# Mamba stage on one core: the two silu activations in one ScalarE block, and the convolution products, norm, gate, residual and output products at other units of the loop body

## What is computed

```python
xz = jnp.einsum('bsd,ed->bse', x, ip_w)
xi, z = jnp.split(xz, 2, axis=-1)
conv = conv_general_dilated(xi.transpose(0, 2, 1), cw, ...) + cb
xi = silu(conv.transpose(0, 2, 1))
dt, Bm, Cm = jnp.split(jnp.einsum('bse,fe->bsf', xi, xp_w), ...)
dt = softplus(jnp.einsum('bsr,er->bse', dt, dtp_w) + dtp_b)
def step(h, t):            # h = exp(dt*A) * h + dt*B*xi,  y = sum_s h*C
    ...
y = ys + xi * Dp
y = y * silu(z)
return jnp.einsum('bse,de->bsd', y, op_w)
```

## Time and profile before

| | value |
|---|---|
| median of three runs | 7089.75 us |
| the profiled execution's own time | 7097.04 us |
| its span | 7095.2 us |
| TensorE, share of the span busy | 88% |
| GpSimd | 66% |
| VectorE | 73% |
| ScalarE | 53% |
| granted TensorE clock, mean | 0.945 of full speed |
| one body of Mamba (36 of them, about 58% of the span) | 114.67 us |

### The profile page before, as it was taken

How to read it: one execution, slowest core, us unless ns; L and a number is a source line. 1 busy time by engine, 2 the same in 40 slices (tenths; PEclk the granted TensorE clock), 3 DMA queues, 4 the chain that set the end, 5 groups by cost and what they waited for, 6 DMA issues and landing times. The chain is left out here.

```text
span 7095.2 us, 72243 instructions
## 1 busy us (share of the span) xinstructions
PE 6238.9 (88%) x19866; PEld 2543.6 (36%) x19866; DVE 5157.7 (73%) x6021; ACT 3746.3 (53%) x6881; POOL 4712.5 (66%) x2193
## 2 busy tenths in 40 slices
PE   8999999999899888889888888888898888888898
PEld 3444444455344233323233322333222333223334
DVE  4444444454222999999999999999999999995623
ACT  4444444422223666666666666666666666664432
POOL 3333333311200999999999999999999999993300
PEclk9999999999999999989899989999898989999998
DMA  2000000100200332324233333323242333332000
GB/s 71 0 0 0 0 0 0 51 10 9 102 0 22 77 82 63 84 72 94 66 82 73 74 95 73 81 64 84 61 105 65 82 73 76 80 82 54 5 0 24
DMA packets 235643, 378.46 MB, mean 53 GB/s; under 512 B 62784, under 2 KB 71680, under 8 KB 233776
## 3 DMA queue, kind: packets, MB, share of 16 engines
q1 hardware_dynamic: 235312, 374.71, 21.7%
HBM read 202.29 MB, written 19.20 MB: 31 GB/s over the span
## 5 line engine op out<-in xcount | busy, mean ns | idle before, releaser
L2413 POOL TENSOR_TENSOR work<-work,weights 128x1024 f32<-128x1024 f32 x1152 | 2692.2, 2362 | 19.9 <-DMA weights<-mamba_bc 12.8
L2272 PE MATMUL banks<-work 128*64 128x512 f32 x4608 | 1370.1, 676 | 600.1 <-POOL work L2418 586.1
L2335 DVE TENSOR_TENSOR_SCAN banks<-banks,work 128x512 f32<-128x512 f32 x1296 | 1622.7, 1276 | 64.4 <-ACT banks L2382 64.3
L2382 ACT ACTIVATE banks<-work 128x512 f32<-128x512 f32 x2304 | 1497.6, 680 | 67.4 <-DVE work L2113 43.1
L2335 DVE TENSOR_TENSOR_SCAN work<-banks,work 128x512 f32<-128x512 f32 x1008 | 1269.2, 1274 | 101.8 <-ACT banks L2382 77.6
L2418 POOL TENSOR_TENSOR work<-work,weights 128x1024 f32<-128x1024 f32 x504 | 1188.4, 2358 | 92.1 <-ACT work L2005 92.1
L1845 PE MATMUL banks<-work,weights 128*128 128x512 f32 (+31 forms) x3796 | 1169.4, 459 | 3.0 <-DVE work L2086 3.0
L555 POOL TENSOR_TENSOR work<-work 128x1024 f32<-128x1024 f32 x256 | 484.1, 1892 | 848.4 <-DVE work L451 848.4
L1845 PEld LDWEIGHTS banks<-work,weights 128*128 128x128 f32 x3796 | 646.1, 193 | 624.9 <-issue 547.2
L2131 DVE TENSOR_TENSOR work<-banks,weights 128x512 f32<-128x512 f32 x1296 | 860.3, 676 | 0.0
L2272 PEld LDWEIGHTS banks<-work 128*64 128x64 f32 x4608 | 266.1, 144 | 1466.6 <-POOL work L2418 884.7
(11 more groups left out here) (297 smaller groups left out, 7568.0 us busy)
## 6 DMA issues: line engine op xcount, KB each, us to landing
weights<-mamba_bc SPq DMA_DIRECT2D x592, 256.0 KB, 5.0
work<-work SPq DMA_DIRECT2D x1160, 128.0 KB, 2.3
weights<-mamba_taps SPq DMA_DIRECT2D x5, 2048.0 KB, 7.4
mamba_taps<-work SPq DMA_DIRECT2D x4, 2048.0 KB, 6.7
work<-in_conv_rows SPq DMA_DIRECT2D x16, 256.0 KB, 6.5
out_T<-X SPq DMA_DIRECT2D x8, 512.0 KB, 3.3
X<-in_xT SPq DMA_DIRECT2D x2, 1536.0 KB, 12.9
weights<-in_in_w SPq DMA_DIRECT2D x5, 512.0 KB, 3.9
```

Of the source, the lines that this page charges most:

```text
L2272: mm = e.matmul(ybank[k % 2][64 * h:64 * h + 64, :], fold, ring_pair(n, j)[:, h, :], start=False, stop=(a == SP_ - 1))
L2335: e.tensor_tensor_scan(ub if by_pool(j) else da, da, ub, state[:, i:i + 1], ALU.mult, ALU.add).then_inc(scanned, 1)
L2382: e.activation(banks[:, slot_of(i), :], dt_rep[:, k % 2, h, :], ACT.Exp, scale=decay[:, f:f + 1]).then_inc(da_full, 1)
L2413: e.tensor_tensor(ring_pair(n, j), u_rep[:, k % 2], bc[:, a, 0, :].unsqueeze(1).to_broadcast([P, 2, TC]), ALU.mult) \
```

## The change

Both silu move into one block behind unit 15, z first and then x, with one return to the other table. TensorE's E3 moves from pairs 2 and 3 of the next body to pairs 26 and 27; E1 from pairs 27 and 28 to pairs 9 and 10 of the same body; E2 from 30 and 31 to 28 and 30; B to 5 and 4; C from 7 to 3. ScalarE copies E0 behind unit 53 (was 59), E1 behind unit 25 (was 3 of the next body), E2 behind 3 (was 9), E3 behind 59 (was 13 of the next body), F0 behind 51 (was 55); the norm's Ln and Exp stand behind units 9 and 11 (were 21 and 23). VectorE's two scales stand ahead of unit 16 (were at 26 and 27), its two residuals too (were at 17 and 19), its last gate ahead of unit 5 (was 7); the product with C of pair 7 comes before unit 16. `load_first` is issued earlier in its body, after a wait for ScalarE's copy of E2.

```diff
-LANE_V = table("E3", "C", "H1", "H2", "F0", "E1")
+LANE_V = table("C", "E1", "H1", "H2", "F0", "E3")
-BEFORE_V, BEFORE_S = table("C", "E1"), table("E0", "E2")
+BEFORE_V, BEFORE_S = table("C", "E1", "E3"), table("E0", "E2")
...
-    E_AT = ((23, 25), (27, 28), (30, 31), (2, 3))
-    G_AT, PE_B, PE_C, PE_H, PE_F = (10, 11), (6, 5), 7, (15, 19), (24, 21, 13, 29)
+    E_AT = ((23, 25), (9, 10), (28, 30), (26, 27))
+    G_AT, PE_B, PE_C, PE_H, PE_F = (10, 11), (5, 4), 3, (15, 19), (24, 21, 13, 29)
...
-    E_OUT, G_OUT, F_OUT, SILU_AT = (59, 3, 9, 13), 29, (55, 49, 33, 1), (15, 7)
+    E_OUT, G_OUT, F_OUT, SILU_AT = (53, 25, 3, 59), 29, (51, 49, 33, 1), 15
...
-        if i == SILU_AT[1]:
+        if i == SILU_AT:
             if N[1] >= 0:
                 e.wait_ge(y_free, y_free_at(N, "F3"))
                 e.wait_ge(ln.v_free, v_at(previous(N), "F0"))
             e.activation(zn, zn, ACT.Silu).then_inc(silu, 1)
-            e.preload_act_table_set("natural_log_exp_and_others")
-        if i == SILU_AT[0]:
-            e.wait_ge(ln.v_free, v_at(N, "E3"))
+            e.wait_ge(ln.v_free, v_at(previous(N), "E3"))
             e.wait_ge(ln.s_free, s_at(previous(N), "E2"))
             e.activation(xi, xi, ACT.Silu).then_inc(silu, 1)
             e.preload_act_table_set("natural_log_exp_and_others")
...
-    SQUARE_AT, RSTD_AT, SCALE_AT = 5, (21, 23), 26
+    SQUARE_AT, RSTD_AT, SCALE_AT = 5, (9, 11), 16
...
-        if i in (SCALE_AT, SCALE_AT + 1):
-            k = i - SCALE_AT
+        for k in range(KD if i == SCALE_AT else 0):
...
-    RESIDUAL = (19, 17)
+    RESIDUAL = (16, 16)
...
+                    if c == CHUNKS - 2:
+                        e.wait_ge(ln.s_free, s_at(previous(N), "E2"))
+                        load_first(e, core, after)
                     e.wait_ge(scanned, scanned_at(N, 15))
                     spread_dt(e, 2)
                     spread_u(e, 2)
-                    if c == CHUNKS - 2:
-                        load_first(e, core, after)
...
-                        if i == 7:
+                        if i == 5:
                             gate(e, previous(N), KI - 1, z[:, (n + 1) % 2])
...
-                        if h == 0 and j > 0 and j - 1 not in SOFT_AFTER and not by_pool(j - 1):
+                        if h == 0 and j > 0 and j - 1 not in SOFT_AFTER + (SILU_AT // 2,) and not by_pool(j - 1):
...
-                        if h == 1 and (j in SOFT_AFTER or j == PAIRS_N - 1) and not by_pool(j):
+                        if h == 1 and (j in SOFT_AFTER + (SILU_AT // 2, PAIRS_N - 1)) and not by_pool(j):
                             e.wait_ge(scanned, scanned_at(N, i))
                             times_c(e, N, n, j, 1)
```

More of the change, by code:

```diff
@@ L1874, in late_pe @@
     def late_pe(e, N, j, c, xi, nb, gone):
[L1876 to L1880, removed]
         if j == PE_B[1]:
@@ L1934, in early_pe @@
             e.wait_ge(ln.s_free, s_before(N, "E0"))
-            e.wait_ge(ln.v_free, v_at(N, "C"))
         if j == E_AT[1][0]:
@@ L1939, in early_pe @@
             e.wait_ge(ln.s_free, s_before(N, "E2"))
+        if j == E_AT[3][0]:
+            e.wait_ge(ln.v_free, v_before(N, "E3"))
         for half in range(2):
@@ L1946, in early_pe @@
                 project_x(e, 2, half, c + 2, lane_s, nb, ln.s_full)
+            if j == E_AT[3][half]:
+                project_x(e, 3, half, c + 2, lane_v, nb, ln.v_full)
     def y_start(e, N, k, xi):
@@ L2016, in late_act @@
             e.activation(zn[:, 3, :], ybank[0], ACT.Copy).then_inc(y_free, 1)
-        if i == E_OUT[1]:
-            e.wait_ge(ln.v_full, v_at(previous(N), "E1"))
-            e.activation(xi[:, 1, :], lane_v, ACT.Identity, bias=lv("conv_b", 1)).then_inc(ln.v_free, 1)
         if i == E_OUT[2]:
@@ L2022, in late_act @@
             e.activation(xi[:, 2, :], lane_s, ACT.Identity, bias=lv("conv_b", 2)).then_inc(ln.s_free, 1)
-        if i == E_OUT[3]:
-            e.wait_ge(ln.v_full, v_at(N, "E3"))
-            e.activation(xi[:, 3, :], lane_v, ACT.Identity, bias=lv("conv_b", 3)).then_inc(ln.v_free, 1)
-        if i == SILU_AT[1]:
+        if i == SILU_AT:
             if N[1] >= 0:
@@ L2075, in early_act @@
             e.activation(lane_v, lane_v, ACT.Exp, scale=-0.5).then_inc(rstd, 1)
+        if i == E_OUT[1]:
+            e.wait_ge(ln.v_full, v_at(N, "E1"))
+            e.activation(xe[:, 1, :], lane_v, ACT.Identity, bias=lv("conv_b", 1)).then_inc(ln.v_free, 1)
+        if i == E_OUT[3]:
+            e.wait_ge(ln.v_full, v_at(N, "E3"))
+            e.activation(xe[:, 3, :], lane_v, ACT.Identity, bias=lv("conv_b", 3)).then_inc(ln.v_free, 1)
         if i == E_OUT[0]:
@@ L2256, in _ @@
                             y_start(e, N, k, x[:, n % 2])
-                        if c == CHUNKS - 2 and j == E_AT[0][0]:
+                        if c == CHUNKS - 2 and j == E_AT[1][0]:
                             e.wait_ge(core.first_loaded, layer * FIRST_LOAD + 2 * FIRST_LOAD)
@@ L2320, in _ @@
                                 gate(e, N, f, z[:, n % 2])
-                        if i == 7:
+                        if i == 5:
                             gate(e, previous(N), KI - 1, z[:, (n + 1) % 2])
-                        for m in range(KD):
+                        for m in (1, 0):
                             if i == RESIDUAL[m]:
@@ L2347, in _ @@
             for m in range(KD):
-                e.wait_ge((ln.s_full, ln.v_full)[m], (s_at(previous(N), "E2"), v_at(previous(N), "E1"))[m] + 1)
+                e.wait_ge((ln.s_full, ln.v_full)[m], (s_at(previous(N), "E2"), v_at(previous(N), "E3"))[m] + 1)
                 xc = chunk(CHUNKS - 1)[:, m, :]
@@ L2384, in _ @@
                             e.wait_ge(core.middle_loaded, layer * MIDDLE_LOAD + 2 * MIDDLE_LOAD)
-                        if c == CHUNKS - 2 and i == E_OUT[0]:
+                        if c == CHUNKS - 2 and i == E_OUT[1]:
                             e.wait_ge(core.first_loaded, layer * FIRST_LOAD + 2 * FIRST_LOAD)
```

## The result

The changed kernel takes **7328.21 us** (7325.41 to 7331.55, four runs) against 7088.62 for the kernel before on the same chip (7087.44 to 7091.39): a ratio of 1.0337, 95% interval 1.0321 to 1.0354, or 239.6 us more. The forecast was 7257 in a range of 7105 to 7335: the sign is right, the time is inside the range, and the loss was put too low by 72 us.

The account below looks back on a forecast made before the run. GpSimd (112.1 of 114.67 us) and VectorE (110.6) were taken as nearly full. E1's line, 65.6 + 15.2 + 38.5, gave a period of 119.3, 4.6 more over 36 bodies: 167 us, so 7257 us, range 7105 to 7335.

Parts of the forecast that it names:

- Bound, and the reach of ScalarE's queue: GpSimd busy 112.1 and VectorE 110.6 of 114.67 us; ScalarE, two pairs ahead, would wait for products taken one or two pairs later.
- Part 1: One silu block behind unit 15: 9.5 us, just covered by VectorE's 9.5 us of work; 3.8 us of VectorE's waits go.
- Part 4: C at pair 3, Ln behind unit 9: q 3 loses 0.2 us; the residuals needing B0 lose nothing.
- Part 2: E0 and F0 copied earlier, units 53 and 51: q 26 begins at 17.1 instead of 14.16, so GpSimd loses 2.9 us.
- Part 3: E3 copied behind unit 59: GpSimd loses 1.1 us more at q 28; E2, F3 and the gate cost nothing.
- Part 5: E1 at pairs 9 and 10, copied behind unit 25: q 8 at 65.6, 15.2 to unit 26, then 38.5: period 119.3 us.
- The size: TensorE's speed after new waits, bounded at periods 118.6 to 121, taken as 119.3: 4.6 us a body, 167 in all.
- Rival (a): Faster: late products find cover, only the silu block's effect is left, GpSimd's 112.1 bounds: 92 us less, 6997 us; chance 0.11.
- Rival (b): Edge of no change: only E1's line holds, q 8 begins 4.2 us earlier; period 115.1, 7105 us; chance 0.07.
- Rival (c): Slower still: TensorE's clock falls for all of B and for E1 too; period 121.5, 7336 us; chance 0.07.
- Rival (d): The silu of x gets its own table load: block 7.7 us, unit 16 late by 1.3, still the forecast; chance 0.01.
- The earlier `load_first`: On SyncE's queue it waits for the copy of E2 (36.9); the loads behind are wanted much later: costs nothing.

Follow-up runs that it names:

- silu_merged: The kernel before with both silu in one block behind unit 15 and one return to the Exp and Ln table, nothing else moved: 7163.03 us, ratio 1.0097.
- gate_back_split: gate_back with the silu of z behind unit 7 and of x behind 15 again, a table return after each: 7022.59 us, ratio 0.9905.
- both_moved: The changed kernel with E0, F0, E2, E3 placed as before, norm behind 11 and 13, E1 at pairs 12 and 13, copied behind unit 33: 7104.74 us.
- e0_e3_later: The changed kernel with F0 copied behind unit 55 (was 51), E0 behind 57 (was 53), E3 behind 63 (was 59): 7327.64 us.
- e1_later: The changed kernel with E1 copied behind unit 31 in place of 25, TensorE's order unchanged: 7219.33 us, ratio 1.0173.
- gate_back: both_moved with the last gate ahead of unit 7 again and E1 copied behind unit 35 in place of 33: 7023.89 us, ratio 0.9908.
- late_as_before: both_moved, but with E1 at pairs 9 and 10 and copied behind unit 25, as in the changed kernel: 7277.14 us, ratio 1.026.
- e1_line_alone: gate_back with E1 at pairs 9 and 10 and copied behind unit 25, as in the changed kernel: 7177.82 us, ratio 1.0121.
- b1_fills: The changed kernel with B1 at pair 3, right behind C, in place of pair 4: 7306.6 us, ratio 1.0302.

## Why the prediction was right, and what it got wrong

- **Bound, and the reach of ScalarE's queue.** Right. Every product that was to be late is late: E0, F0, E3, C, E1 in 33 or 34 of 34 bodies.
- **Part 1, the block is covered.** Right in the changed kernel, where no scan waits at unit 16. Its sum was added wrongly: 1.3, 6.4, 0.2 and 0.65 are 8.6 us and not 9.5, so the cover had nearly a microsecond to spare; the trace has 8.9, from the end of pair 5's scans (2694.86) to the end of unit 16's Exp (2703.7). What waits there is the residual for B0, 1.1 us a body (38.1 in all), which Part 4 put at nothing: B was counted at TensorE's full speed, though the text had bounded its half speed. What the block is worth was put too high: 2.57 us a body if alone, down to GpSimd's bound. Alone it lost 1.8, E3's wait included (silu_merged), and with the other places mended it is worth nothing (gate_back_split).
- **Part 2, E0.** 2.9 us at q 26 against 2.4 on average; alone 4.3 us a body against 4.55. The half of E0 that was taken at 5.07 us, after the row before, takes 3.7 to 3.9 in 32 of the 34 bodies now. That row was one draw of several: in the kernel before, this half takes 3.7 to 3.9 us in 14 of 34 bodies and 4.3 to 5.6 in 20.
- **Part 3, E3.** 1.1 at q 28, measured 1.2 on average. The gate and the copies of F3 and E2 "at nothing" were right only because VectorE was late, as that part said, with 2 to 3 us as the price if the cover went. It went in both_moved (gate, 3.2) and in e0_e3_later (F3 and E2).
- **Part 5, E1's line.** The sum was 65.6 us from the end of q 22 to q 8, 15.2 from q 8 to unit 26 and 38.5 from there to the end of q 22. The 34 bodies have 65.8, 16.6 and 38.5 on average. The first agrees by two errors that offset each other, which is luck: q 28 comes 0.3 us earlier than the 25.1 said, as E0 is faster, and feed 11 waits 0.9 us for TensorE, put at nothing. The second is short by 1.4. The part also didn't see that E1 delays G, hidden behind E1's own copy until e1_later moved that away.
- **The size.** The term that fell short is E1's half in that line: it was summed at 3.64 us, the full clock, and takes 4.5 to 5.8 in 27 of 34 bodies. The forecast had a term for the clock, but at B, ahead of sum 3, and the "1.4 lost, of which 1.1 is spare" behind it was read from E0's half, which is fast now. 36 bodies at 1.59 more (120.89 less 119.3) are 57 of the 72 us that were short. The ends of the stage, which the sum left out, are 8. The 7 left lie in the kernel before: its profiled execution, 7097.04, was 8.4 us above the median of its four runs, and the profiled one of the changed kernel 0.8.
- **The bodies differ.** Of the 34 bodies 18 take 119.7 to 120.2 us, 5 take 120.8 to 121.0, 8 take 121.5 to 121.9, and the first of a layer 122 to 127.6, the longest where the hardware loop turns. The kernel before isn't even either: most of its bodies take 114.2 to 114.4, some 114.8 to 115.9, and the one at the turn 119.2, so 114.67 is a mean.
- **Rival (a), faster by 92 us,** did not happen in the changed kernel. With the late products given cover, gate_back takes 7023.89 (body 112.35), within 27 us of its 6997. The rule of the Trainium skill ("ScalarE: Activation LUTs", section "Table sets: the hidden batching unit") is to batch by table set; here two table loads a body against four differ by 1.3 us of 7023, less than the runs can tell, since ScalarE is not the bound. The drain that the Trainium skill ("ScalarE: Activation LUTs", section "What ACT_TABLE_LOAD costs") adds to a load is in no row: the silu starts 0.01 us behind the load, and in silu_merged 2675.33 is right behind 2674.04 + 1.28.
- **Rival (b)** had the mechanism right: E1's line alone has q 8 at 61.4 us, 4.2 earlier, just as it said. Its size was too low, 115.1 against 116.8, for the same reason as the forecast's: 15.2 at the full clock against 16.9.
- **Rival (c),** the low clock for all of B and for E1 too, came nearer than the forecast: 7336 against 7328, where the forecast is 71 off. It is half true: E1 is slow in 27 bodies of 34, and of B only B1, in 30 (4.3 to 5.9 us).
- **Rival (d)** did not happen: a body has two table loads (L2022 and L2026, 34 each in 34 bodies), and the silu of x has none.
- **The earlier `load_first`** cost nothing that shows: no engine waits over 0.6 us for a transfer in these bodies.

## What to carry to other kernels

Where an engine serves several others in one hand-written order, each duty's place is a due time: put it where its input is surely made, and count that in the producer's queue, not in pairs of one's own. When such a place is moved, one wait covers the next: undoing one of two causes gave nothing here (e0_e3_later), and a move that looked harmless, the gate two units earlier, cost 12 us in the kernel before and 99 in a schedule where the late part was mended (late_as_before against e1_line_alone). So read who waits after every step. A lighter load on ScalarE, 60% busy, was worth nothing by itself. And when a forecast takes a duration from one body, look at the same row in the others: E0's half took 3.7 us in some and 5.4 in others, and the forecast saw one of them.

## What the runs showed of the hardware

TensorE's granted clock over the 34 bodies is 0.89 in the changed kernel and 0.92 in gate_back and in the kernel before, though TensorE does the same work in all three. Idle stretches of 3.29 us (changed kernel) and 4.85 us (b1_fills) were followed by work that took 5.62 for 3.70 and 4.47 for 3.64. Idle time alone does not settle it: behind nearly the same idle time, half of E1 ran at full speed in one body and slowly in the next (timeline of TensorE in the changed kernel, the body of 119.70; the row for the next is above, 5.40 behind 2.04):

```profile
2592.04 1.08 PE L2268 MATMUL banks<-work 128*64 128x512 f32 x4 [2.02 <-POOL work L2415]
2593.05 3.71 PE L1845 MATMUL banks<-work,weights 128*128 128x512 f32 x12
```

So bodies with the same work differ by 1.8 us (119.7 and 121.5). The two levels are 1.2 and 2.4 GHz. The granted clock is 1.00 over the fast half and 0.68 over the slow one, and in both bodies it is 1.00 through the idle stretch ahead and the sum between: in the slow one it falls while TensorE is busy with the half itself, after the idle stretch has ended. Ahead of sum 3 it falls within the idle stretch already (0.84 over it, 0.50 over the sum). Why the one body kept the high level and the other did not stays open.
